# A decoder layer on one core: second batch's first attention moved in the fill, new orders of fill, loop and finish, loop written out

## The chip, the cores and the metric

The kernel runs on one core of a Trainium2 chip. The metric is the device time of one execution in microseconds (us), the median of several. The core has five engines that each work through their own queue of instructions in order: TensorE (PE, matrix products and transposes into PSUM), VectorE (DVE), ScalarE (ACT), GpSimd (POOL) and SyncE (SP, which here only issues DMAs). They meet through semaphores alone, so the order in which instructions stand in each queue is part of the program.

## What is computed

One pre-norm decoder layer over 16 batches of 256 tokens with 256 features: self-attention (16 heads of 16), cross-attention to 77 context tokens, and a soft mixture as the feed-forward (FFN), each added to its input.

```python
x = x + attn(layernorm(x))                    # 16 heads, softmax over 256 keys
x = x + xattn(layernorm(x), ctx, ctx, mask)   # 16 heads, softmax over 77 keys
# FFN: xn = rms_norm(layernorm(x)); se = rms_norm(slot_embeds)  (8 x 128 = 1024 slots)
logits   = einsum('bsd,etd->bset', xn, se)
dispatch = softmax(logits, axis=1)            # over the tokens
slots    = einsum('bsd,bset->betd', xn, dispatch)
h        = gelu(slots @ w1) @ w2              # 256 -> 1024 -> 256
combine  = softmax(logits over all 1024 slots)
x = x + einsum('bnd,bsn->bsd', h, combine)
```

## The kernel before

**Steps and prefixes.** All work is cut into some 60 named steps, each a short function per engine. A prefix tells the part: `c` is self-attention (xt.1, q, k, v, then four softmax rounds scores.n, mt.n, shifted.n, pv.n, then tr, ob, oproj), `d` is cross-attention (xt.2, kv, q2, two rounds scores2, mt2, shifted2, pv2, then tr2, ob2, oproj2) with the FFN's logits (xt.3, logits.0 to 3), `m` is the FFN in four chunks of 256 slots (lt, dispatch, slots, hidden.c.0 to 3, outer.c.0 and 1, comb, combine) and `l` its last chunk's rest, run one iteration later. In a name of the fill a number is the batch: `c1` is the second batch's self-attention. `s` are one-time steps; `s0.idle.n` is n 128x128 matmuls of the identity (line L852) whose result nobody reads.

**Order.** What stands behind what on each engine is written out by hand as lists of such names, one list per engine: START (the fill: c0 to c2, d0, d1, m0), ORDER (one iteration of the loop: c of batch b+2, d of b+1, m of b, l of b-1, 13 times, a hardware loop over `b` in `program`) and FINISH (the last two FFNs and the last cross-attention).

**A softmax round.** scores.n on PE (8 matmuls into PSUM banks 1 to 4), row maxima on DVE (`mx`, L1122, then a small copy L1125), a transpose of the maxima on PE (mt), its two halves on ACT (`mh`) and DVE (`sh`, L1130), the products again, shifted, on PE (L560, L564), exp on ACT (L895), and pv on PE (L577). The banks 1 to 4 go from user to user in a written ring, QUAD: a user may begin when the one before it has done its exp. Bank 0 goes round in a ring MISC for all short products. Banks 5 to 7 belong to the FFN: slots in 5, hidden and the transposes in 5 and 6, outer and combine in 7. c's q, k and v go to banks 1, 2 and 3 and are a user of QUAD (`c.qkv`).

**FFN precision.** Products are made of three fp32r matmuls each (`three`, L455 to L457: high x high, low x high, high x low), so each operand has a high half (ACT) and a low half (DVE, L1045 and L1255; for the hidden layer POOL, L1372). The chain of one chunk is lt, column maximum (DVE L1234), exp (ACT L955), norm (DVE L1238, L1241), dispatch, halves (ds), slots, halves (sl), hidden, gelu (ACT L991), halves (h_hi, h_lo), outer, halves (pr), combine, sum (acc).

Of the kernel before, what the change touches and what calls it, by code (L numbers as in the profile page):

```python
# [7 lines left out]
H, HD = 16, 16  # L8
# [40 lines left out]
        m.lt.0 l.outer.3.0 m.dispatch.0 d.xt.2 l.outer.3.1 c.xt.1 m.slots.0 l.comb.3 d.kv c.q m.hidden.0.0 c.k d.q2  # L49
        c.v m.hidden.0.1 d.scores2.0 m.hidden.0.2 m.hidden.0.3 m.lt.1 d.mt2.0 l.combine.3 d.shifted2.0 m.outer.0.0  # L50
        m.dispatch.1 c.scores.0 d.pv2.0 m.outer.0.1 c.mt.0 m.slots.1 m.comb.0 c.shifted.0 m.hidden.1.0 m.hidden.1.1
        c.pv.0 d.scores2.1 d.tr2.0 m.hidden.1.2 d.ob2.0 m.hidden.1.3 d.mt2.1 m.lt.2 m.combine.0 d.shifted2.1
        m.outer.1.0 m.dispatch.2 c.scores.1 d.pv2.1 m.outer.1.1 c.mt.1 m.slots.2 m.comb.1 c.shifted.1 m.hidden.2.0
# [20 lines left out]
    """,
    pool="""
        d.rstd.2 c.rstd.1 m.hid.0.0 m.hid.0.1 d.bias.2 m.hid.0.2 m.hid.0.3 m.hid.1.0 c.bias.1 m.hid.1.1 m.hid.1.2
# [6 lines left out]
        s0.idle.10 c0.xt.1 s0.idle.14 c0.q c0.k c0.v c0.scores.0 s0.idle.8 c0.mt.0 s0.idle.4 c0.shifted.0 s0.idle.6  # L83
        c0.scores.1 c0.pv.0 s0.idle.8 c0.mt.1 s0.idle.2 c0.shifted.1 s0.idle.6 c0.pv.1 s0.idle.2 c0.tr.0 c0.scores.2
        s0.idle.8 c0.ob.0 s0.idle.2 c0.mt.2 s0.idle.4 c0.shifted.2 s0.se_transp.0 s0.idle.4 c0.scores.3 c0.pv.2
        s0.idle.8 c0.mt.3 s0.idle.4 c0.shifted.3 s0.idle.4 s0.se_transp.1 c0.pv.3 s0.idle.2 c0.tr.1 s0.idle.2 c0.ob.1
        s0.idle.2 c0.oproj s0.idle.20 d0.xt.2 s0.idle.12 c1.xt.1 s0.idle.6 d0.kv c1.q c1.k d0.q2 c1.v s0.idle.4
        d0.scores2.0 s0.idle.12 d0.mt2.0 s0.idle.6 d0.shifted2.0 s0.idle.10 c1.scores.0 d0.pv2.0 s0.idle.8 c1.mt.0
        s0.idle.4 c1.shifted.0 s0.idle.2 d0.tr2.0 s0.idle.6 d0.scores2.1 c1.pv.0 s0.idle.2 d0.ob2.0 s0.idle.4
        d0.mt2.1 s0.idle.2 d0.shifted2.1 s0.idle.10 c1.scores.1 d0.pv2.1 s0.idle.8 c1.mt.1 s0.idle.2 c1.shifted.1  # L90
        s0.idle.2 d0.tr2.1 s0.idle.4 c1.pv.1 s0.idle.2 c1.tr.0 c1.scores.2 d0.ob2.1 s0.idle.2 d0.oproj2 c1.ob.0
        s0.idle.2 c1.mt.2 s0.idle.4 c1.shifted.2 s0.idle.8 c1.scores.3 c1.pv.2 s0.idle.8 c1.mt.3 s0.idle.2
        c1.shifted.3 s0.idle.8 c1.pv.3 s0.idle.2 d0.xt.3 s0.idle.4 d0.logits.0 d0.logits.1 d0.logits.2 d0.logits.3
        c1.tr.1 m0.lt.0 c1.ob.1 s0.idle.4 c1.oproj m0.dispatch.0 s0.idle.4 m0.slots.0 s0.idle.2 m0.hidden.0.0
        m0.hidden.0.1 d1.xt.2 m0.hidden.0.2 c2.xt.1 m0.hidden.0.3 d1.kv c2.q c2.k d1.q2 c2.v m0.lt.1 d1.scores2.0
        m0.outer.0.0 d1.mt2.0 m0.dispatch.1 d1.shifted2.0 m0.slots.1 m0.comb.0 c2.scores.0 d1.pv2.0 m0.outer.0.1
        c2.mt.0 m0.hidden.1.0 c2.shifted.0 d1.tr2.0 m0.hidden.1.1 d1.scores2.1 c2.pv.0 m0.hidden.1.2 d1.ob2.0
        d1.mt2.1 m0.lt.2 m0.hidden.1.3 d1.shifted2.1 m0.combine.0 m0.dispatch.2 c2.scores.1 d1.pv2.1 m0.slots.2
        c2.mt.1 m0.comb.1 c2.shifted.1 m0.outer.1.0 c2.pv.1 c2.scores.2 d1.tr2.1 m0.outer.1.1 d1.ob2.1 m0.hidden.2.0
        c2.tr.0 m0.hidden.2.1 d1.oproj2 m0.hidden.2.2 c2.ob.0 m0.hidden.2.3 m0.lt.3 c2.mt.2 m0.combine.1 c2.shifted.2  # L100
        m0.outer.2.0 m0.dispatch.3 c2.scores.3 c2.pv.2 m0.slots.3 m0.comb.2 c2.mt.3 m0.outer.2.1 c2.shifted.3
        m0.hidden.3.0 m0.hidden.3.1 c2.pv.3 m0.hidden.3.2 d1.xt.3 m0.combine.2 m0.hidden.3.3 d1.logits.0 d1.logits.1
# [3 lines left out]
        c0.xt.1 s0.hi.0 s0.hi.1 c0.q c0.mh.0 c0.ex.0 s0.se_squares c0.xo.0 c0.mh.1 c0.ex.1 c0.xo.1 c0.od.0 c0.mh.2
        c0.ex.2 c0.xo.2 c0.mh.3 s0.hi.2 s0.se_hi.0 c0.ex.3 c0.xo.3 s0.hi.3 c0.od.1 d0.xt.2 c1.xt.1 c1.q s0.se_hi.1
        d0.q2 d0.mh2.0 d0.ex2.0 d0.xo2.0 c1.mh.0 s0.hi.4 c1.ex.0 c1.xo.0 d0.od2.0 d0.mh2.1 d0.ex2.1 d0.xo2.1 c1.mh.1
        c1.ex.1 c1.xo.1 d0.od2.1 c1.od.0 c1.mh.2 c1.ex.2 c1.xo.2 c1.mh.3 c1.ex.3 c1.xo.3 d0.xt.3 d0.logits.0
# [1425 lines left out]
```

## Time and profile before

| | us |
|---|---|
| median of 3 runs (1885.05 to 1885.58) | 1885.53 |
| the profiled execution's own time | 1885.74 |
| its span, first to last instruction | 1883.9 |
| PE busy in the span | 1817.1 (96%) |
| DVE, ACT, POOL busy | 1071.3, 969.7, 426.4 |
| fill, to the loop's first instruction on PE | 258.6 |
| loop, 13 iterations | 1449.7 |
| finish | 175.6 |

The profile is one execution read by the hardware profiler. Its page gives each engine's busy time and the costliest groups of instructions. The trace behind it answers questions: instructions in order of time, who waited for whom, busy time by stretch. Rows of PE overlap a little, since matmuls are pipelined and their ends are modelled. An x16 on an fp32 product of 8 matmuls, or x20 on 10 fillers, is right: each shows as two.

### The profile page before, as it was taken

The numbers are of one execution on the slowest core, as the hardware profiler recorded it, in microseconds if no ns is written. First come the engines' busy times: TensorE is split into PE (matmuls) and PEld (weight loads), VectorE is DVE, ScalarE is ACT, GpSimd is POOL, SyncE is SP. The second block draws the span as 40 slices with busy tenths as digits, with TensorE's granted clock in tenths as the row PEclk, the third lists the DMA queues.
The fourth block names the chain that finished last, engine by engine and source line by source line (L and its number), as shares of the span: only waits on it lengthen the run. The fifth ranks groups of instructions, "written<-read, shape, count | busy, mean of one in ns | idle before, by whom it ended". The sixth has DMA issues, their size and how long they took to land.

```text
span 1883.9 us, 42647 instructions
## 1 busy us (share of the span) xinstructions
PE 1817.1 (96%) x17464; PEld 1621.7 (86%) x17464; DVE 1071.3 (57%) x2211; ACT 969.7 (51%) x1711; POOL 426.4 (23%) x351
## 2 busy tenths in 40 slices
PE   8999999999999999999999999999999999999998
PEld 7878898898989889898888989889898988989888
DVE  3445565665655556565665656556565655655453
ACT  3334646555454554555455554555546455555653
POOL 2011222221221222121222122122122122212232
PEclk9999999999999999999999999999999999999999
DMA  4000000000000000000000000000000000000000
GB/s 153 9 1 9 2 10 7 7 9 1 15 1 7 9 2 15 1 9 7 7 9 1 15 1 10 7 7 9 1 15 1 9 7 7 9 1 7 1 7 6
DMA packets 20842, 19.75 MB, mean 10 GB/s; under 512 B 9920, under 2 KB 19776, under 8 KB 20288
## 3 DMA queue, kind: packets, MB, share of 16 engines
q1 hardware_dynamic: 20672, 17.06, 3.2%
q8 instruction: 158, 2.59, 0.6%
q14 instruction: 12, 0.10, 0.0%
HBM read 12.86 MB, written 4.19 MB: 9 GB/s over the span
## 4 chain that ended last, share of the span: by engine, by line
PE 66%; issue 19%; DVE 7%; POOL 5%; ACT 3%; POOLq 0%; DMA 0%; DVEq 0%; SPq 0%; ACTq 0%
PE ps L455 14%; PE ps L457 13%; PE ps L456 13%; POOL h_lo L1372 4%; PE ps L540 3%; PE ps L852 3%; PE ps L577 2%; PE ps L671 2%; PE ps L717 2%; PE ps L687 2%; PE ps L652 1%; PE ps L760 1%; DVE h_hi L1255 1%; POOL pw_d L1356 1%; DVE sl_lo L1045 1%
## 5 line engine op out<-in xcount | busy, mean ns | idle before, releaser
L1372 POOL TENSOR_TENSOR h_lo<-h_f,h_hi 128x512 fp32r<-128x512 f32 x256 | 331.6, 1297 | 1120.5 <-DVE h_hi L1255 1120.5
L455 PE MATMUL ps<-sl_hi,w_hi 128*128 128x256 f32 x1024 | 302.3, 295 | 11.8 <-DVE cb_lo L1045 9.9
L455 PE MATMUL ps<-w_hi,h_hi 128*128 128x256 f32 x1024 | 301.3, 294 | 3.9 <-POOL h_lo L1372 3.9
L456 PE MATMUL ps<-w_hi,h_lo 128*128 128x256 f32 x1024 | 290.0, 283 | 0.0
L457 PE MATMUL ps<-w_lo,h_hi 128*128 128x256 f32 x1024 | 290.0, 283 | 0.0
L456 PE MATMUL ps<-sl_hi,w_lo 128*128 128x256 f32 x1024 | 289.1, 282 | 0.0
L457 PE MATMUL ps<-sl_lo,w_hi 128*128 128x256 f32 x1024 | 289.0, 282 | 0.0
L1255 DVE CAST h_hi<-h_f 128x512 fp32r<-128x512 f32 x256 | 132.6, 520 | 218.1 <-ACT h_f L991 217.6
L991 ACT ACTIVATE h_f<-ps 128x512 f32<-128x512 f32 x256 | 152.4, 596 | 136.4 <-PE ps L457 135.3
L1122 DVE TENSOR_REDUCE mx<-ps 128x8 f32<-128x2048 f32 x64 | 146.5, 2289 | 131.8 <-PE ps L540 131.8
L455 PEld LDWEIGHTS ps<-w_hi,h_hi 128*128 128x128 f32 x1024 | 196.0, 191 | 29.0 <-issue 24.1
L455 PEld LDWEIGHTS ps<-sl_hi,w_hi 128*128 128x128 f32 x1024 | 194.8, 190 | 25.5 <-issue 20.4
L456 PEld LDWEIGHTS ps<-w_hi,h_lo 128*128 128x128 f32 x1024 | 196.5, 192 | 0.0
L457 PEld LDWEIGHTS ps<-w_lo,h_hi 128*128 128x128 f32 x1024 | 196.3, 192 | 0.0
L456 PEld LDWEIGHTS ps<-sl_hi,w_lo 128*128 128x128 f32 x1024 | 195.4, 191 | 0.1
L457 PEld LDWEIGHTS ps<-sl_lo,w_hi 128*128 128x128 f32 x1024 | 195.1, 191 | 0.0
L895 ACT ACTIVATE pt<-ps 128x2048 f32<-128x2048 f32 x64 | 120.4, 1881 | 47.6 <-PE ps L564 47.6
L866 ACT ACTIVATE xo<-ps 128x512 f32<-128x512 f32 (+1 forms) x96 | 43.7, 455 | 150.7 <-PE ps L687 92.5
L866 ACT ACTIVATE mh<-ps 128x512 fp32r<-128x512 f32 (+1 forms) x96 | 43.6, 454 | 99.0 <-PE ps L549 84.2
L991 ACT ACT_TABLE_LOAD x67 | 86.0, 1283 | 10.3 <-PE ps L457 9.1
L866 ACT ACTIVATE od<-ps 128x256 f32<-128x256 f32 x64 | 24.6, 384 | 122.8 <-PE ps L596 70.1
L866 ACT ACTIVATE pr_hi<-ps 128x512 fp32r<-128x512 f32 x64 | 38.3, 599 | 89.0 <-PE ps L457 89.0
(202 smaller groups left out, 4225.8 us busy)
## 6 DMA issues: line engine op xcount, KB each, us to landing
x<-in_x SPq DMA_DIRECT2D x16, 256.0 KB, 2.7
out<-acc SPq DMA_DIRECT2D x16, 256.0 KB, 2.2
g_w<-in_w SPq DMA_DIRECT2D x2, 1024.0 KB, 11.4
...
```

What stands on the lines that cost most here:

```text
L455: te.matmul(o, lhs[0], rhs[0], start=first, stop=False)
L456: te.matmul(o, lhs[1], rhs[0], start=False, stop=False)
L457: return te.matmul(o, lhs[0], rhs[1], start=False, stop=last)
L540: last = te.matmul(ps[:, 1 + i, t * S:(t + 1) * S], q[rows, c, t * P:(t + 1) * P], km[rows, e, c, :], start=True, stop=True)
L577: last = te.matmul(ps[32 * i:32 * i + 32, 0, 0:S], vz[:, j, 8 * c + 2 * i + e, :], pt[:, i, j, :], start=j == 0, stop=j == NT - 1)
L852: te.matmul(ps[:, 7, 0:P], ident[:, :], ident[:, :], start=True, stop=True)
L866: return nc.scalar.activation(o, i, ACT.Copy)
L895: nc.scalar.activation(pt[:, :, :, :].rearrange("p i j s -> p i (j s)"), ps[:, 1:1 + R, :], ACT.Exp)\
L991: nc.scalar.activation(h_f[:, 2 * q:2 * q + 2, :], halves(hidden_bank(b, q)), ACT.Gelu).then_inc(s["ge"], 1)
L1122: V.tensor_reduce(mx[:, n, :, :], ps[:, 1:1 + R, :].rearrange("p i (t s) -> p i t s", t=NT), AX, ALU.max, negate=True).then_inc(s["mx"], 1)
L1255: V.tensor_copy(h_hi[:, 2 * q:2 * q + 2, :], h_f[:, 2 * q:2 * q + 2, :]).then_inc(s["h_hi"], 1)
L1372: Q_.tensor_tensor(h_lo[:, part, :], h_f[:, part, :], h_hi[:, part, :].bitcast(f32), ALU.subtract)\
```

## The change

What it does:

- **Fill.** c1's q, k and v go to banks 5, 6 and 7 instead of 1 to 3 (`qkv_bank`), which the FFN has not used yet, and leave the ring QUAD. Their evictions on ACT and DVE get one wait more each (for c0's last products), and the first batch's lt, slots and outer wait for them (`km`, `q_sb`, `v_sb` of batch 1). In QUAD_START d0's two users now stand ahead of all four of c1's, and d0's logits ahead of c1's third and fourth. c1's steps stand later, d0's and m0's earlier. The fillers go from 276 to 183. The slot embeddings' transposes (se_transp) are cut from two steps over two banks into four over bank 5.
- **All three lists** of PE, ACT, DVE and POOL are new; k now stands ahead of q. Each holds the same steps as before, save those split ones and the fillers. nrm and nrm2 wait for ob and ob2 of the half before.
- **The loop** of 13 iterations is a Python loop: the same instructions, written out one after another, with constants in the waits instead of registers.

PE in the fill, from c0's oproj on (L607 before, L613 after; L852 and L865 are the fillers, L497 and L500 xt, wkv the step kv). Before:

```order
L607 MATMUL ps<-wo,od 128x256 x4
L852 MATMUL ps<-consts 128x128 x20
L497 MATMUL ps<-consts,xh_d 128x128 x4
L852 MATMUL ps<-consts 128x128 x12
L497 MATMUL ps<-consts,xh_a 128x128 x4
L852 MATMUL ps<-consts 128x128 x6
L618 MATMUL ps<-wkv_61,cx 77x256 x2
L621 MATMUL ps<-cx,wkv_61 128x77 x4
L455 MATMUL ps<-xa_hi,wqk_hi 128x256
```

After:

```order
L613 MATMUL ps<-wo,od 128x256 x4
L857 MATMUL ps<-consts,g_se 128x128 x4
L865 MATMUL ps<-consts 128x128
L624 MATMUL ps<-wkv_61,cx 77x256 x2
L627 MATMUL ps<-cx,wkv_61 128x77 x4
L865 MATMUL ps<-consts 128x128 x8
L500 MATMUL ps<-consts,xh_d 128x128 x4
L857 MATMUL ps<-consts,g_se 128x128 x4
L865 MATMUL ps<-consts 128x128 x3
L458 MATMUL ps<-xd_hi,wq_hi 128x256
```

c1's transpose (xh_a) and its projections (wqk) are gone from between d0's xt.2 and d0's q2, and 26 fillers less stand there.

DVE in the fill, from d0's first row maxima on (mx_107, md_108, sh_110, rl_112 are cross-attention's tiles; mx, md, sh self-attention's). Before:

```order
L1177 TENSOR_REDUCE mx_107<-ps 128x16
L1180 COPY md_108<-mx_107 128x32
L1186 SCALAR_TENSOR_TENSOR sh_110<-mh_109,consts,ps 128x512
L1122 TENSOR_REDUCE mx<-ps 128x8
L1125 COPY md<-mx 128x16
L1130 SCALAR_TENSOR_TENSOR sh<-mh,consts,ps 128x256
L1193 RECIPROCAL rl_112<-ps 128x16
L1196 TENSOR_TENSOR on_113<-ps,rl_112 128x8x16 x2
L1177 TENSOR_REDUCE mx_107<-ps 128x16
```

After:

```order
L1198 TENSOR_REDUCE mx_107<-ps 128x16
L1201 COPY md_108<-mx_107 128x32
L1106 TENSOR_SCALAR xh_a<-x,mv,pw 128x256 x2
L1207 SCALAR_TENSOR_TENSOR sh_110<-mh_109,consts,ps 128x512
L1060 TENSOR_TENSOR xa_lo<-ps,xa_hi 128x512
L1198 TENSOR_REDUCE mx_107<-ps 128x16
```

c1's first softmax round (L1122, L1130) no longer stands between d0's two rounds.

PE in the loop, from the FFN's lt.3 (tile lg) to dispatch.3 (tile edt); wo_63 is oproj2. Before:

```order
L751 MATMUL ps<-consts,lg 128x128 x4
L717 MATMUL ps<-wo_63,od_114 128x256 x4
L455 MATMUL ps<-pr_hi,cb_hi 128x256
...
L549 MATMUL ps<-consts,md 128x128 x2
L760 MATMUL ps<-consts,edt 128x128 x4
```

After:

```order
L759 MATMUL ps<-consts,lg 128x128 x4
L723 MATMUL ps<-wo_63,od_114 128x256 x4
L566 MATMUL ps<-q,km 128x256 x4
L570 MATMUL ps<-sh,ones 128x256 x4
...
L583 MATMUL ps<-pt,vz 32x256 x8
L458 MATMUL ps<-w_hi,h_hi 128x256
...
L593 MATMUL ps<-consts,xo 128x128 x4
L768 MATMUL ps<-consts,edt 128x128 x4
```

Where combine.1 (12 matmuls) stood behind oproj2, shifted.2, pv.1, outer.2.0 (24 matmuls) and tr.0 stand now, and combine.1 stands earlier.

The core of the diff; of the lists, only the loop's PE list around the place above is shown. In order: the list, the ring, the loop, `qkv_bank` and its users on PE, the new waits of the first lt, slots and outer, those of the evictions of c1's q, k and v, those of nrm and nrm2 (the same two lines with ob2's semaphore), and SyncE's loop:

```diff
-        c.pv.1 c.scores.2 d.tr2.1 m.hidden.2.1 d.ob2.1 m.hidden.2.2 c.tr.0 m.hidden.2.3 c.ob.0 m.lt.3 d.oproj2
-        m.combine.1 c.mt.2 m.dispatch.3 c.shifted.2 m.comb.2 m.slots.3 c.scores.3 c.pv.2 m.outer.2.0 c.mt.3
+        m.hidden.2.1 d.tr2.1 c.scores.2 m.combine.1 d.ob2.1 m.hidden.2.2 c.mt.2 m.hidden.2.3 m.lt.3 d.oproj2
+        c.shifted.2 c.pv.1 m.outer.2.0 c.tr.0 m.dispatch.3 c.scores.3 c.pv.2 m.slots.3 m.comb.2 c.mt.3 m.outer.2.1
...
 QUAD_START = """
-    c0.qkv c0.quad.0 c0.quad.1 c0.quad.2 c0.quad.3 c1.qkv d0.oct.0 c1.quad.0 d0.oct.1 c1.quad.1 c1.quad.2 c1.quad.3
-    d0.logits c2.qkv d1.oct.0 c2.quad.0 d1.oct.1 c2.quad.1 c2.quad.2 c2.quad.3 d1.logits
+    c0.qkv c0.quad.0 c0.quad.1 c0.quad.2 c0.quad.3 d0.oct.0 d0.oct.1 c1.quad.0 c1.quad.1 d0.logits c1.quad.2
+    c1.quad.3 c2.qkv c2.quad.0 d1.oct.0 d1.oct.1 c2.quad.1 c2.quad.2 c2.quad.3 d1.logits
...
     run_list(steps, START[engine])
-    with handle.Fori(1, B - 2) as b:
-        run(engine, steps, c=b + 2, d=b + 1, m=b, l=b - 1)
+    for b in range(1, B - 2):
+        run(steps, ORDER[engine], c=b + 2, d=b + 1, m=b, l=b - 1)
     run_list(steps, FINISH[engine])
...
+        def qkv_bank(a, k):
+
+            return (5, 6, 7)[k] if second_batch(a) else 1 + k
...
             def q_step(a):
 
+                if second_batch(a):
+                    pe.wait_ge(s["i_slo"], 2 * ND)
...
             def k_step(a):
 
                 split(a, "wqk")
-                quad_free("c.qkv", a)
+                if not second_batch(a):
+                    quad_free("c.qkv", a)
                 pe.wait_ge(s["xt1_lo"], nth("xt1_lo", a, 1))
...
+                    if not later(b):
+                        pe.wait_ge(s["km"], nth("km", 1, 1))
...
+                    if not later(b):
+                        pe.wait_ge(s["q_sb"], nth("q_sb", 1, 1))
...
+                    else:
+                        pe.wait_ge(s["v_sb"], nth("v_sb", 1, 1))
...
+                if second_batch(a):
+                    act.wait_ge(s["st_ps"], nth("st_ps", a - 1, Q))
...
+                if second_batch(a):
+                    dve.wait_ge(s["st_ps"], nth("st_ps", a - 1, Q))
...
+                if second_batch(a):
+                    dve.wait_ge(s["pv"], nth("pv", a - 1, Q))
...
+                if c:
+                    dve.wait_ge(s["ob_ps"], nth("ob_ps", a, c))
...
-            with sp.Fori(1, B - 3) as b:
+            for b in range(1, B - 3):
```

## Rows read from the trace of the kernel before

**Rows 1.** The page: busy us, share of the span, instructions, by engine.

```profile
PE 1817.1 (96%) x17464; PEld 1621.7 (86%) x17464; DVE 1071.3 (57%) x2211; ACT 969.7 (51%) x1711; POOL 426.4 (23%) x351
```

**Rows 2.** Stretches from:to, length, busy us by engine, PE clock: fill, loop, finish.

```profile
3.85:258.61 254.76, 241.31 (x2380) 208.72 (x2381) 122.96 (x258) 111.13 (x181) 44.47 (x34) 1.00 0.10 31
...
258.61:1708.34 1449.73, 1415.87 (x13730) 1261.08 (x13729) 860.79 (x1781) 770.82 (x1365) 333.81 (x273) 1.00 0.03 7
1708.34:1883.90 175.56, 159.95 (x1357) 151.89 (x1355) 87.10 (x171) 86.47 (x164) 45.61 (x35) 0.99 0.02 6
```

**Rows 3.** Groups of instructions: busy us, mean ns, idle before; the fillers.

```profile
L852 PE MATMUL ps<-consts 128*128 128x128 f32 x552 | 74.4, 285 | 3.9 <-DMA consts<-in_consts 3.9
```

**Rows 4.** PE by time (start, us, line, tiles): c0's scores.0, .1, .3.

```profile
17.84 1.15 PE L540 MATMUL ps<-km,q 32*128 32x256 f32 x16 [1.16 <-DVE vz L1115]
...
26.46 1.15 PE L540 MATMUL ps<-km,q 32*128 32x256 f32 x16 [0.44 <-ACT pt L895]
...
46.08 1.15 PE L540 MATMUL ps<-km,q 32*128 32x256 f32 x16
```

**Rows 5.** The same view: c0.oproj, d0.scores2.0, d0.oproj2, d0.logits.0, m0.hidden.0.0.

```profile
59.09 1.96 PE L607 MATMUL ps<-wo,od 128*128 128x256 f32 x8
...
79.06 0.41 PE L645 MATMUL ps<-mk_r,ones 1*128 1x308 f32 x4
...
120.63 1.97 PE L717 MATMUL ps<-wo,od 128*128 128x256 f32 x8
...
141.54 0.47 PE L455 MATMUL ps<-se_hi,xd_hi 128*128 128x512 f32 x1 [0.57 <-issue]
...
156.62 0.39 PE L455 MATMUL ps<-sl_hi,w_hi 128*128 128x256 f32 x1 [0.97 <-DVE sl_lo L1045]
```

**Rows 6.** PE's waits: us in all, times, longest; first two loop only, then all.

```profile
PE ps L760 <- DVE edt L1241: 15.9, 13, 1.2
...
PE ps L455 <- DVE cb_lo L1045: 9.2, 26, 0.4
...
PE ps L497 <- DVE xh_d L1091: 3.4, 13, 0.3
PE ps L824 <- DVE ds_lo L1045: 2.5, 13, 0.2
```

**Rows 7.** PE by time: two FFN matmuls in a row; lt.3 and dispatch.3 of one iteration.

```profile
280.67 0.28 PE L456 MATMUL ps<-sl_hi,w_lo 128*128 128x256 f32 x1
280.79 0.28 PE L457 MATMUL ps<-sl_lo,w_hi 128*128 128x256 f32 x1
...
780.27 0.60 PE L751 MATMUL ps<-consts,lg 128*128 128x128 f32 x4
...
785.78 0.66 PE L760 MATMUL ps<-consts,edt 128*128 128x128 f32 x4 [1.23 <-DVE edt L1241]
```

**Rows 8.** DVE and POOL by time: row maxima of d's round 0, their copy; copy of round 1.

```profile
726.76 1.44 DVE L1177 TENSOR_REDUCE mx<-ps 128x16 f32<-128x1232 f32 x1
...
728.08 1.29 POOL L1366 TENSOR_TENSOR x<-x,biases 128x512 f32<-128x512 f32 x1
...
728.24 1.18 DVE L1180 COPY md<-mx 128x32 f32<-128x32 f32 x1
...
753.92 0.20 DVE L1180 COPY md<-mx 128x32 f32<-128x32 f32 x1
```

**Rows 9.** PE's waits in the finish.

```profile
PE ps L455 <- POOL h_lo L1372: 3.9, 3, 1.8
PE ps L760 <- DVE edt L1241: 1.8, 1, 1.8
```

**Rows 10.** Code fetches from 400 to 512 us (packets, MB, engines' share); PE across an iteration's end.

```profile
q8 instruction: 10, 0.16, 0.7%
...
814.52 1.89 PE L607 MATMUL ps<-wo,od 128*128 128x256 f32 x8
816.26 0.65 PE L751 MATMUL ps<-consts,lg 128*128 128x128 f32 x4
```

More of the change, by code:

```diff
@@ L48 @@
     pe="""
[L49 to L53, printed above, removed]
@@ L82 @@
     pe="""
[L83 to L102, printed above, removed]
@@ new lines @@
+        s0.idle.3 c0.ob.1 s0.idle.2 c0.oproj s0.se_transp.1.0 s0.idle.1 d0.kv s0.idle.8 d0.xt.2 s0.se_transp.1.1
+        s0.idle.3 d0.q2 s0.idle.4 d0.scores2.0 s0.idle.8 d0.mt2.0 s0.idle.6 d0.shifted2.0 c1.xt.1 s0.idle.6
+        d0.scores2.1 d0.pv2.0 c1.k d0.mt2.1 c1.q d0.shifted2.1 d0.tr2.0 c1.v d0.ob2.0 c1.scores.0 d0.pv2.1 s1.idle.3
+        d0.tr2.1 s1.idle.4 c1.mt.0 s1.idle.4 d0.ob2.1 c1.shifted.0 d0.oproj2 s1.idle.1 c1.scores.1 c1.pv.0 s1.idle.6
+        c1.mt.1 s1.idle.5 c1.shifted.1 s1.idle.3 d0.xt.3 s1.idle.7 d0.logits.0 d0.logits.1 d0.logits.2 d0.logits.3
@@ new lines @@
+        s1.idle.3 m0.lt.0 c1.scores.2 c1.pv.1 s1.idle.6 c1.mt.2 s1.idle.2 m0.dispatch.0 c1.shifted.2 c1.tr.0
+        m0.slots.0 c1.ob.0 c1.scores.3 c1.pv.2 m0.hidden.0.0 c1.mt.3 m0.hidden.0.1 c1.shifted.3 d1.kv m0.hidden.0.2
+        s1.idle.1 c1.pv.3 s1.idle.2 c1.tr.1 m0.hidden.0.3 c1.ob.1 m0.lt.1 c1.oproj m0.outer.0.0 m0.dispatch.1 d1.xt.2
+        m0.outer.0.1 c2.xt.1 m0.slots.1 m0.comb.0 c2.k c2.q c2.v m0.hidden.1.0 c2.scores.0 d1.q2 m0.hidden.1.1
+        c2.mt.0 m0.hidden.1.2 c2.shifted.0 m0.hidden.1.3 d1.scores2.0 c2.pv.0 m0.lt.2 d1.mt2.0 m0.combine.0
@@ new lines @@
+        d1.shifted2.0 m0.outer.1.0 m0.dispatch.2 d1.scores2.1 d1.pv2.0 m0.outer.1.1 d1.mt2.1 m0.slots.2 m0.comb.1
+        d1.shifted2.1 d1.tr2.0 m0.hidden.2.0 d1.ob2.0 c2.scores.1 m0.hidden.2.1 m0.hidden.2.2 c2.mt.1 m0.hidden.2.3
+        d1.pv2.1 c2.shifted.1 m0.lt.3 d1.tr2.1 m0.combine.1 d1.ob2.1 c2.scores.2 c2.pv.1 m0.dispatch.3 d1.oproj2
+        m0.comb.2 c2.mt.2 m0.slots.3 c2.shifted.2 m0.outer.2.0 c2.tr.0 c2.scores.3 c2.pv.2 m0.outer.2.1 c2.mt.3
+        m0.hidden.3.0 c2.shifted.3 d1.xt.3 m0.hidden.3.1 m0.hidden.3.2 m0.combine.2 c2.pv.3 d1.logits.0 c2.ob.0
@@ L104 @@
+        m0.hidden.3.3 c2.tr.1 d1.logits.1 d1.logits.2 c2.ob.1 d1.logits.3 c2.oproj
     """,
     act="""
[L106 to L109, printed above, removed]
```

298 lines of the change are left out of this document (154 added, 144 removed).

## The prediction

> **What bounds the kernel.** The page's busy times come first: PE works 1817.1 of 1883.9 us, DVE 57%, ACT 51% [rows 1]. Where PE has work ready, a matmul of 256 columns follows the last after 0.12 us [rows 7]. So the kernel can get shorter only where PE idles or does work that nobody reads. The second view, three stretches side by side, shows where that is [rows 2]: fill 254.76 us with 241.31 busy; loop 1449.73 with 1415.87 busy, so 33.9 idle, 2.6 in each of 13 iterations of 111.5; finish 175.56 with 159.95 busy. The third, the groups of instructions, shows that the fill's 241.31 are no real load: 276 fillers take 74.4 of it, 0.27 us each [rows 3]. The fill's length is set by chains of dependent steps across the engines. Its marks on PE, read from the instructions in time, are c0.oproj 59.09, d0.scores2.0 79.06, d0.oproj2 120.63, d0.logits.0 141.54, m0.hidden.0.0 156.62 [rows 5] and the loop's start 258.61 [rows 2].
>
> The sum is made against the profiled execution's 1885.74 us (span 1883.9 and 1.8 outside it); the median, 1885.53, is 0.2 lower.
>
> **Fill.** Six legs, one mark to the next. One turn of the ring of banks (scores, maxima, mt, shifted, exp) takes 26.46 - 17.84 = 8.62 us [rows 4].
>
> 1. To c0.oproj, 59.09. The fourth round begins at 46.08 now, behind se_transp.0 and fillers; three bare turns behind the first it would begin at 17.84 + 3 x 8.62 = 43.7. In the new list scores.3 has tr.0 and 5 fillers ahead of it and se_transp is cut in four. I take the bare turn: -2.4, oproj at 56.7.
> 2. To scores2.0, 19.97 now. Ahead of it 26 fillers go (26 x 0.27 = 7.0) and c1's xt.1, q, k, v. These are 4 transposes and 36 matmuls at 0.12, some 4.9 us, part of which now only fills a wait for d0's projections; with both gone the chain oproj, x1, statistics, xh, transpose, q2 is left bare. I take -8.6, leaving 11.4: less than the 11.9 taken out, because the bare chain then binds. scores2.0 at 68.0.
> 3. To oproj2, 41.57 now. c1.quad.0 and c1.quad.1 leave the ring between d0's users: two turns of about 8.6 less, and 0.8 comes back where c1's q, k and v stand between d0's steps. I take -16.4, leaving 25.2; oproj2 at 93.2.
> 4. To logits.0, 20.9 now, with c1.quad.2 and quad.3 in the ring ahead of it; now the bank ring puts one c1 turn there (quad.1, with quad.0 begun before oproj2). One turn less: -8.8, logits.0 at 105.3.
> 5. To hidden.0.0, 15.1 now. c1's scores.2, shifted.2, mt.2 and scores.3 stand inside this leg, 0.6 to 1.2 each, beside the exp and norm that bind it: +2.6, hidden.0.0 at 123.
> 6. To the loop, 102.0 now. This stretch is matmul-bound already; c1's last round, tr.1, ob.1 and oproj move into it, which is 8 fp32 matmuls each of shifted, pv and oproj beside small ones, 4.7 us, and 1.0 of new waits: +5.7, loop at 231.
>
> Sum -2.4 - 8.6 - 16.4 - 8.8 + 2.6 + 5.7 = -27.9; I take **-27**. Another road bounds it: 93 fillers less are 93 x 0.27 = 25.1 us, and the fill idles 254.76 - 241.31 = 13.5 now, so more than -31 would need nearly half that idle gone too. The low end, -22, has two things the walk may have wrong: POOL's s0.lo.4 stands just ahead of d0.rstd.2, and ACT's s0.hi.4 and s0.se_hi.1 near od.1 and xt.2; each is a weight's half that took no path before. No row prices their meeting; the nearest, the DVE copy below that met POOL and took 1.0 longer [rows 8], would put it at 1 us a meeting, five of them at 5.
>
> **Loop.** PE's waits, grouped by what ended them [rows 6], give 31 of the 33.9 us idle less the small ones. Four groups are broken by the new order:
> dispatch.3 on the norm (edt), 15.9 in 13: lt.3 begins at 780.27 and dispatch.3 at 785.78, 5.5 us of chain of which 1.23 is wait [rows 7]. The new order puts oproj2 (1.7, a 1.97 with its overlap [rows 5]), shifted.2 and pv.1 (1.3 and 1.0, like the 1.15 of scores [rows 4]), outer.2.0 (24 x 0.12 = 2.9 [rows 7]) and tr.0 (0.4) there, with lt itself 8 us: the chain is covered, -15.9.
> hidden.1.0 and 2.0 on cb_lo, 9.2 in 26: outer.0.1 and outer.1.1 (2.9 each) now stand between comb and it. -9.2.
> xt.2 on xh_d, 3.4 in 13: xt.2 now stands behind slots.0, some 5 us later, against a longest wait of 0.3. -3.4.
> comb.2 on ds_lo, 2.5 in 13: scores.3, pv.2 and slots.3 stand between. -2.5.
> These are 31.0, 2.4 an iteration. PE also pays at each wait for the lost overlap of pipelined matmuls; the spans in a row show 0.28 for a start each 0.12 [rows 7], so up to 0.16 per wait, of which there are some five an iteration: 0.8 more at most. Against it stand the new waits. I walked one iteration's four queues with the durations of the trace. shifted.3 finds sh.3 0.2 late, since d.xt.3 (0.4) took over from longer work; on DVE d.mx2.0 now stands ahead of hid.0.1 to 0.3 and of cm.1, so POOL's casts (1.3 each, as the 1.29 row [rows 8]) end with 0.5 to spare for outer.0.0; some ten more links have under 0.1. I put them at 0.3 where they add, and take back 0.2 of the overlap's 0.8: 2.4 + 0.2 - 0.3 = 2.3 an iteration, **-30**, period 109.2. Upper bound: all of 33.9 and the overlap, -41. Lower bound: each of the ten tight links 0.1 late, 1.0, and a copy's 1.0 worse each iteration: 2.3 - 2.0, -4; I hold -12 for the range, since not all links can be on the path at once.
>
> The last of these bounds has its row: DVE's copy after the maxima took 1.18 us where POOL's tensor operation had begun 0.16 before it, and 0.20 where not [rows 8]. In the new order the same copy comes some 1 us after POOL's operation ends, by my walk. The Trainium skill, "SBUF — State Buffer", section "SBUF: two separate sides", calls the port pair that the two share an exclusive lock held for a whole instruction; the trace agrees, with 1.29 against 1.18. By that rule, if the order shifts the copy by a microsecond, the loop would lose 1.0 x 13 = 13 us of the 30.
>
> Written out, the loop has the same instructions and no branch. Code comes at 10 packets in 112 us, 0.7% of 16 engines, so 0.007 x 16 x 112 / 10 = 1.25 us each [rows 10]. PE passes an iteration's end from c.oproj at 814.52 to lt at 816.26: 1.74 for a matmul group that lasts 1.89, no gap [rows 10]. I take 0. The added waits for c1's q, k, v and for ob are on things long done (oproj of c0 is 13 us ahead of c1's eviction by the marks): 0, bounded by the smallest wait group above, 0.2 each.
>
> **Finish.** dispatch.3 of the last but one FFN waits 1.8 on edt [rows 9]; oproj2 and outer.2.0 (1.7 + 2.9) now stand ahead of it: -1.8. The last FFN's outer.0.0 waits for POOL's h_lo, a part of the 3.9 in three [rows 9], 1.3; it moves behind dispatch.2: -1.2. The end stays. **-3**, between -6 (all 5.7 of both rows) and 0.
>
> **Sum.** 1885.7 - 27 - 30 - 3 = 1825.7, or **1825.5** against the median.
>
> **Rivals.** *A, the forecast*, 0.72; own range 1812 (ends -31, -37 and -6) to 1840.
> *B, the loop's waits only change places.* The order is a balance of four queues; ten links with under 0.1 to spare speak for it, and that idle is only 2.6 an iteration. Against it speaks that the covers are 2 to 3 us where the waits are 0.2 to 1.2. Then 1885.5 - 27 - 3 = 1855.5. 0.16.
> *C, the branch had a price.* If each engine had to fetch the loop's first code anew at each turn, writing it out would save 13 x 1.25 = 16 us more: about 1809. No gap at the iteration's end speaks against it. 0.04. The Trainium skill, "Runtime: NRT & Kernel Launch", section "Instruction fetch mechanics", says that a taken branch to code outside the current window must fetch before it goes on, and that full unrolling is preferred for it; the 1.74 us above do not show it.
> *D, the change doesn't do what it says in the fill*: d0's chain is as long without c1's turns, since the engines' own chain binds it, not the ring. Then only loop and finish remain, 1885.5 - 33 = 1852.5. Against it, 41.57 us for two cross-attention rounds is nearly five turns. 0.05.
> *E, slower: code comes late.* At 10 packets per 112 us the span needs about 168; if the written-out code were not fetched ahead, each would stop its engine for 1.25 us: 168 x 1.25 = 210 us, time 1885.5 - 60 + 210 = 2035. It decides from 60 / 1.25 = 48 packets on, 2 in 7. Against it: fill and finish are straight code already, and the fill idles 13.5 us in 2380 groups of matmuls [rows 2], too little for late code. 0.03.
>
> **Numbers.** Faster by over 0.2% (3.8 us, about what a measurement of this kernel tells from no change): A, B, C, D less a sliver, 0.95. Same 0.02, slower 0.03. The range 1812 to 1852 leaves out C, E, and most of B, 0.2 together.
>
> **What would show it.** PE's marks: c0.oproj about 57, scores2.0 68, oproj2 93, logits.0 105, hidden.0.0 123, loop from 231. Leg 3 is the test of the ring: if it is still over 35, D holds. 183 fillers. A period of 109.2, with no wait on edt or cb_lo and under 0.6 us of PE idle an iteration; if the idle is over 2 under other names, B. Finish 172. Code packets at the same rate; gaps of 1 us in several engines that nothing in the trace ends would be E, a period below 108 would be C. The forecast is wrong above all if the hand walk missed a link: one 1 us link in the loop is 13 us.

## The result, and the profile after

The changed kernel takes 1810.32 us (median of 4 runs, 1810.08 to 1810.62) against 1885.55 (4 runs, 1885.05 to 1885.74): ratio 0.9601, 95% interval 0.9585 to 0.9618. That is 75.2 us less, where 60 were forecast, and 1.7 us below the low end of the range.

The page of after, its busy line (compare [rows 1]), and, in the second block, the three stretches, cut at the same steps as [rows 2] (from:to, length, busy us with counts for PE, PEld, DVE, ACT, POOL, then PE clock, DMA share, GB/s):

```profile
PE 1781.7 (99%) x17278; PEld 1596.0 (88%) x17278; DVE 1062.4 (59%) x2213; ACT 970.0 (54%) x1713; POOL 429.9 (24%) x351
```

```profile
3.70:233.02 229.32, 220.72 (x2194) 187.39 (x2195) 124.16 (x260) 116.39 (x187) 44.40 (x34) 1.00 0.11 34
233.02:1637.82 1404.80, 1402.99 (x13730) 1258.15 (x13729) 850.49 (x1781) 770.15 (x1366) 337.89 (x274) 1.00 0.03 7
1637.82:1808.50 170.68, 158.03 (x1357) 150.49 (x1355) 87.27 (x171) 82.16 (x160) 45.14 (x35) 1.00 0.02 6
```

The loop began at 258.61 and begins at 233.02: 25.6 us less. The loop went from 1449.73 to 1404.80 with the same 13730 matmul records: 44.9 less, a period of 108.06 instead of 111.5. The finish went from 175.56 to 170.68: 4.9 less. The sum is 75.4 of span. PE's busy time in the loop fell only from 1415.87 to 1402.99, so 32 of the 44.9 us were idle on record and 13 were not. What is left of idle in the loop is 1.8 us in all.

PE in order of time (start, us, engine, line, tiles), the marks of the fill and the seam of two iterations of the loop; in the second block the fillers' group (183 fillers, 50.8 us):

```profile
56.71 0.46 PE L613 MATMUL ps<-wo,od 128*128 128x256 f32 x1
...
68.50 0.42 PE L651 MATMUL ps<-mk_r,ones 1*128 1x308 f32 x4
...
94.03 0.48 PE L723 MATMUL ps<-wo,od 128*128 128x256 f32 x1
...
107.17 0.47 PE L458 MATMUL ps<-se_hi,xd_hi 128*128 128x512 f32 x1
...
125.02 0.39 PE L458 MATMUL ps<-sl_hi,w_hi 128*128 128x256 f32 x1
...
772.85 0.59 PE L613 MATMUL ps<-wo,od 128*128 128x256 f32 x2
773.28 0.38 PE L759 MATMUL ps<-consts,lg 128*128 128x128 f32 x2
```

```profile
L865 PE MATMUL ps<-consts 128*128 128x128 f32 x366 | 50.8, 287 | 3.7 <-DMA consts<-in_consts 3.7
```

Against [rows 5] the first five are c0.oproj (59.09 before), scores2.0 (79.06), oproj2 (120.63), logits.0 (141.54) and hidden.0.0 (156.62). The next view, PE's waits over the whole span by what ended them, has nothing of edt left, and cb_lo and xh_d only outside the loop:

```profile
PE ps L458 <- POOL h_lo L1396: 4.6, 6, 2.1
PE ps L865 <- DMA consts<-in_consts: 3.7, 1, 3.7
PE ps L500 <- DVE xh_d L1106: 1.7, 2, 1.2
PE ps L458 <- DVE sl_lo L1060: 1.5, 2, 1.0
...
PE ps L458 <- DVE cb_lo L1060: 0.4, 1, 0.4
```

### The profile page after: what moved, and what is told of

Its sections match the earlier page's. It is cut to its first block, busy times and chain, and to the rows that moved or that the text cites. A ratio compares the mean times of both kernels' runs of the same rounds, so it can differ in the third digit from the quotient of the medians.

```text
span 1808.5 us, 40567 instructions
## 1 busy us (share of the span) xinstructions
PE 1781.7 (99%) x17278; PEld 1596.0 (88%) x17278; DVE 1062.4 (59%) x2213; ACT 970.0 (54%) x1713; POOL 429.9 (24%) x351
## 4 chain that ended last, share of the span: by engine, by line
PE 91%; DVE 4%; POOL 3%; ACT 2%; issue 1%; DMA 0%; POOLq 0%; DVEq 0%; SPq 0%; ACTq 0%
PE ps L458 22%; PE ps L459 20%; PE ps L460 20%; PE ps L546 4%; PE ps L566 3%; POOL h_lo L1396 3%; PE ps L583 2%; PE ps L677 2%; PE ps L693 2%; PE ps L836 2%; PE ps L658 2%; PE ps L768 1%; PE ps L613 1%; PE ps L759 1%; PE ps L500 1%; DVE h_hi L1278 1%
## 5 line engine op out<-in xcount | busy, mean ns | idle before, releaser
L1396 POOL TENSOR_TENSOR h_lo<-h_f,h_hi 128x512 fp32r<-128x512 f32 x256 | 336.2, 1323 | 1125.8 <-DVE h_hi L1278 1125.8
L1278 DVE CAST h_hi<-h_f 128x512 fp32r<-128x512 f32 x256 | 156.7, 622 | 118.0 <-ACT h_f L1006 117.6
L1060 DVE TENSOR_TENSOR ds_lo<-ps,ds_hi 128x512 fp32r<-128x512 f32 x64 | 44.1, 688 | 90.5 <-ACT ds_hi L879 90.4
L879 ACT ACTIVATE ds_hi<-ps 128x512 fp32r<-128x512 f32 x64 | 38.2, 597 | 104.3 <-PE ps L768 104.2
L970 ACT ACTIVATE edt<-ps,cm 128x256 f32<-128x256 f32 x128 | 59.6, 470 | 60.6 <-DVE cm L1257 58.9
```

Of the source, the lines that this page charges most:

```text
L879: return nc.scalar.activation(o, i, ACT.Copy)
L970: last = nc.scalar.activation(edt[:, e, :], ps[:, 6, e * S:(e + 1) * S], ACT.Exp, bias=cm[:, k:k + 1], accum_out=csum[:, k:k + 1])
L1278: V.tensor_copy(h_hi[:, 2 * q:2 * q + 2, :], h_f[:, 2 * q:2 * q + 2, :]).then_inc(s["h_hi"], 1)
L1396: Q_.tensor_tensor(h_lo[:, part, :], h_f[:, part, :], h_hi[:, part, :].bitcast(f32), ALU.subtract)\
```

## The experiments

Each run was measured together with the kernel before on the same chip, and that one's median was 1885.8 to 1886.3, against 1885.55 above. So medians of different runs can be set side by side to about 1 us. The letters are the theories of the expectations, and C is the prediction's rival.

**Is it the order or the writing out?** First the two changes to the loop one at a time. e1 is the kernel before with Python loops, e2 the changed kernel with the hardware loop, e3 the kernel before with the loop's new lists.

```diff
# e1, on the kernel before (e2 is the same in reverse, on the changed kernel)
-    with handle.Fori(1, B - 2) as b:
+    for b in range(1, B - 2):
...
-            with sp.Fori(1, B - 3) as b:
+            for b in range(1, B - 3):
# e3, on the kernel before: ORDER, MISC and QUAD of the changed kernel, and in nrm (nrm2 alike)
+                if c:
+                    dve.wait_ge(s["ob_ps"], nth("ob_ps", a, c))
```

> The kernel before with its loop written out in Python, every list as before. Theory W (what a wait costs PE is its recorded idle plus the overlap that the pipelined matmuls lose at it, 3.44 us an iteration in all; branch, registers and code fetch cost nothing): 1885.5, within 1. Rival H (the 0.84 us an iteration by which the loop got shorter beyond its recorded idle came from the hardware loop's branch and register waits): 1885.5 - 11 = 1874.6. The prediction's rival C: 1869.

> The changed kernel with the hardware loop put back on all engines, orders as in the changed one. Theory W: 1810.3, within 1, period 108.06. Rival H: 1810.3 + 11 = 1821, period 108.9. Rival C: 1826.

> The kernel before with the loop's four lists, both bank rings of the loop and nrm's wait as in the changed kernel; fill, finish and the hardware loop as before. Theory W: the whole loop gain and nothing else, 1885.5 - 44.9 = 1840.6, within 2 for the two seams; PE's period 108.06 and no idle in it. Rival H: 0.84 an iteration stays, 1851.5, period 108.9. If the fill's new end is needed for a loop without waits (its steps reach the loop late otherwise), the first iterations are longer than the rest.

Measured: e1 1886.7 against 1885.9, ratio 1.0001 (0.9992 to 1.0011): writing out the old order does nothing. e2 1843.4: in the changed kernel the hardware loop costs 33 us. e3 1864.7: the new order in a hardware loop brings 21.2 of the 44.9. By e3's trace its loop takes 1428.8 us against 1404.8, so behind the old fill the hardware loop costs 24. The branch is taken 12 times: 2.75 us each in e2, 2.0 in e3. What makes the two differ was not found; 6.1 us of gaps inside outer.3.0 stand in e2 alone. No theory foresaw any of this: H and C priced the branch alike in both orders, W at nothing. PE's waits from the second to the last iteration, in e3 and in e2 (us in all, times, longest), then the seam in e2:

```profile
PE ps L753 <- issue: 19.6, 12, 1.9
```

```profile
PE ps L767 <- issue: 19.7, 12, 1.9
PE ps L468 <- issue: 6.1, 8, 1.0
```

```profile
780.27 0.38 ACT L887 ACTIVATE od<-ps 128x256 f32<-128x256 f32 x1
...
781.23 1.89 PE L621 MATMUL ps<-wo,od 128*128 128x256 f32 x8
784.86 0.65 PE L767 MATMUL ps<-consts,lg 128*128 128x128 f32 x4 [1.74 <-issue]
```

L753 and L767 are lt, the first step behind the branch. "issue" says that no semaphore released it. Before, the same seam had none: 814.52, then 816.26 [rows 10]. Here lt comes 4.2 us after od.1 (780.65), the last thing that a step ahead of the branch waits for. In the kernel before there were 5.3 us from od.1's end (810.99) to lt, so a price of about 4.2 could lie under work that PE had queued.

The DMA view agrees that code is fetched there. In e2, e3, e5, e9 and the kernel before, one packet of instructions moves 2.6 to 3.0 us ahead of lt at each of the 19 seams looked at (in e2, 2.9 ahead of 784.86; in the kernel before, 2.9 ahead of 816.26); at seven seams of e1 and of the changed kernel none moves between 4 and 2 us ahead of it. So the fetch is there in the kernel before too, under matmuls. No run changes the fetch alone, so that it is what lt waits for rests on this timing.

e5 tests whether queued work can cover the price: in e2, od.1 early again.

```diff
-        d.logits.1 d.logits.2 d.logits.3 c.ob.1 m.combine.2 c.oproj
+        d.logits.1 c.ob.1 d.logits.2 d.logits.3 m.combine.2 c.oproj
...
-        m.ge.3.3 m.ec.3 d.logits.0 d.logits.1 d.logits.2 d.logits.3 c.od.1
+        m.ge.3.3 c.od.1 m.ec.3 d.logits.0 d.logits.1 d.logits.2 d.logits.3
```

> As e2 (changed orders, hardware loop), with c.ob.1 moved ahead of logits.2 on PE and c.od.1 ahead of ec.3 on ACT, so that what c.oproj, the last step before the branch, waits for is done some 5 us before PE needs it, as in the kernel before (od.1 ended 5.3 us ahead of the next lt there, 4.2 in e2). Theory Q (PE's sequencer may not go past the wait of c.oproj early; only what PE still has queued by then covers the fetch behind the branch): the 1.74 us gap at lt goes, 1843.4 - 13 x 1.9 = 1819; 1812 if outer.3.0's stretch (4.36 instead of 3.12 us) goes too. Rival D (the branch empties PE's queue and costs the same wherever the waits are; the order before hid it otherwise): 1843.

Measured 1825.6: 17.8 us less, so where the wait stands does matter and rival D is out; but the gap only shrank. PE's waits in the loop, and the seam:

```profile
PE ps L766 <- issue: 8.2, 12, 1.0
```

```profile
775.02 1.89 PE L620 MATMUL ps<-wo,od 128*128 128x256 f32 x8
777.84 0.54 PE L766 MATMUL ps<-consts,lg 128*128 128x128 f32 x3 [0.93 <-issue]
```

od.1 now ended at 771.41, 6.4 us ahead of lt, and yet 0.68 us is left on average. So time since the last wait isn't all; what differs still from before is which matmuls stand last: combine.2 of 256 columns instead of logits of 512. e9 puts these last.

```diff
-        d.logits.1 c.ob.1 d.logits.2 d.logits.3 m.combine.2 c.oproj
+        d.logits.1 c.ob.1 m.combine.2 d.logits.2 d.logits.3 c.oproj
```

> As e5 (changed orders, hardware loop, od.1 early), with combine.2 moved ahead of logits.2, so that logits.2, logits.3 (6 matmuls of 512 columns each, 1.37 us) and c.oproj stand last before the branch, as in the kernel before. Theory Q2 (before a branch PE's sequencer can be ahead by a fixed number of instructions, not by a time; about 20 matmuls. In e5 the last 20 are oproj and combine.2, 1.7 + 1.4 = 3.2 us, against 4.2 from the last wait to lt in e2; before, they are oproj and two logits, 4.5 us): the gap at lt goes, 1825.6 - 13 x 1.0 = 1812.5. Rival D2 (a fixed cost of about 1 us is left in any order that has no slack elsewhere): 1825.

Measured 1822.4, not 1812.5. The gap at lt did go: "issue" fell from 8.2 us in 12 to one of 0.3, elsewhere.

```profile
PE ps L465 <- DVE pr_lo L1067: 2.2, 11, 0.2
PE ps L467 <- issue: 0.3, 1, 0.3
```

```profile
1211.01 1.89 PE L620 MATMUL ps<-wo,od 128*128 128x256 f32 x8
1213.03 0.54 PE L766 MATMUL ps<-consts,lg 128*128 128x128 f32 x3
```

The run is slower than expected because combine.2, now earlier, waits for pr_lo (0.2 each, and 0.16 of overlap lost with it), lt still begins 2.02 us after oproj where 1.74 is bare, and from lt to kv it takes 3.66 us instead of 3.31. These add to 1.0, and the period (109.01) is 0.95 above 108.06. The fixed number of instructions in Q2 fits three kernels' seams (none, 0.68, near none), but a queue's depth was only inferred from them; the 0.35 behind lt was not taken apart.

**What a wait costs.** e6 puts one long wait back into the changed kernel, e13 a short one.

```diff
# e6
-        c.shifted.2 c.pv.1 m.outer.2.0 c.tr.0 m.dispatch.3 c.scores.3
+        c.shifted.2 m.dispatch.3 c.pv.1 m.outer.2.0 c.tr.0 c.scores.3
# e13
-        m.slots.0 d.xt.2 c.k c.q m.hidden.0.0 d.q2
+        m.slots.0 d.xt.2 c.k m.hidden.0.0 c.q d.q2
```

> The changed kernel with dispatch.3 moved ahead of pv.1, outer.2.0 and tr.0 in the loop's PE list, so that it waits for the norm again: edn.3 ends at 744.5, shifted.2 would end at 742.6. Theory W (a wait costs its recorded idle and 0.16 to 0.25 of lost overlap): idle about 1.9 recorded, period longer by 2.1, 1810.3 + 13 x 2.1 = 1838. Rival I (a wait costs what is recorded, as the prediction all but took it): period longer by just the recorded idle. The comparison of period and recorded idle decides, whatever the wait's size is.

Measured 1844.8, 34.5 more than the changed kernel, 2.65 an iteration. PE's waits in iterations 2 to 12, and the stretches of four iterations (as above):

```profile
PE ps L768 <- DVE edt L1264: 21.3, 11, 2.0
```

```profile
234.09:345.66 111.57, 109.63 (x1057) 97.74 (x1056) 65.32 (x137) 59.48 (x106) 26.23 (x22) 0.98 0.03 7
345.66:455.69 110.03, 108.09 (x1057) 96.75 (x1056) 65.20 (x137) 59.11 (x105) 25.98 (x21) 1.00 0.03 7
455.69:567.23 111.54, 109.61 (x1058) 97.85 (x1057) 65.32 (x137) 59.11 (x105) 25.96 (x21) 0.98 0.03 7
567.23:677.26 110.03, 108.09 (x1057) 96.75 (x1056) 65.29 (x137) 59.11 (x105) 25.98 (x21) 1.00 0.03 7
```

The wait is 1.94 each. Iterations at clock 1.00 are 1.97 longer than 108.06; those at 0.98, 6 of 13, are 3.5 longer: right behind the wait, in the 3.7 us from 314.01 on, the granted clock is 0.54 of full, so nearly all of it at TensorE's lower level of 1.2 GHz instead of 2.4; pv.1 and outer.2.0 take 1.5 us more. No theory had that. The period by itself doesn't separate W from I, since a small wait of outer.2.0 vanished with the move: it now begins 1.00 us after pv.1's start, and 1.20 in the changed kernel. With this 0.20 put back, the wait of 1.94 costs 2.17, W's 2.1 and not I's 1.94.

> The changed kernel with hidden.0.0 moved ahead of c.q in the loop's PE list. It then waits for sl_lo, which ends some 0.65 us after c.k does. Theory W (price is recorded idle plus the overlap of 0.16 us that the pipelined matmuls have without a wait): recorded 0.65, period longer by 0.81, 1810.3 + 10.5 = 1820.8, clock 1.00 throughout. Rival I (price is the recorded idle): period longer by 0.65, 1818.8. Rival S (the later steps make it up): 1810.

Measured 1822.5, and 1811.1 for the changed kernel beside it: 11.3 more, 0.87 an iteration. PE's waits in 12 iterations, one iteration's hidden.0.0, the granted clock over most of the loop; then the same place in the changed kernel:

```profile
PE ps L458 <- DVE sl_lo L1060: 7.6, 12, 0.6
```

```profile
681.44 0.39 PE L458 MATMUL ps<-sl_hi,w_hi 128*128 128x256 f32 x1 [0.63 <-DVE sl_lo L1060]
```

```profile
366.00:1528.00 1162.00, 1154.08 (x11321) 1031.06 (x11320) 696.88 (x1453) 635.57 (x1124) 274.83 (x223) 1.00 0.03 7
```

```profile
679.04 0.28 PE L460 MATMUL ps<-xa_lo,wqk_hi 128*128 128x256 f32 x1
679.16 0.28 PE L458 MATMUL ps<-sl_hi,w_hi 128*128 128x256 f32 x1
```

The period went from 108.06 to 108.97, 0.91, for 0.63 of recorded idle. Of the other 0.28, 0.16 is the overlap (a matmul starts 0.12 after the last one, whose record is 0.28 long), and 0.11 is the first matmul behind the wait, 0.39 instead of 0.28. I and S are out; W has the right mechanism and is too small.

**The fill.** e7 drops all fillers of the changed kernel (every `idle` name from START's PE list), e8 halves them in the kernel before, e10 puts c1's projections back into the ring.

```diff
# e8 (each n of s0.idle.n halved, rounded down)
-        s0.idle.10 c0.xt.1 s0.idle.14 c0.q c0.k c0.v c0.scores.0 s0.idle.8 c0.mt.0
+        s0.idle.5 c0.xt.1 s0.idle.7 c0.q c0.k c0.v c0.scores.0 s0.idle.4 c0.mt.0
# e10, on the changed kernel (on ACT c1.q, on DVE c1.k also stand one place later)
-            return (5, 6, 7)[k] if second_batch(a) else 1 + k
+            return 1 + k
...
-                if not second_batch(a):
-                    quad_free("c.qkv", a)
+                quad_free("c.qkv", a)
...
-    c0.qkv c0.quad.0 c0.quad.1 c0.quad.2 c0.quad.3 d0.oct.0 d0.oct.1 c1.quad.0
+    c0.qkv c0.quad.0 c0.quad.1 c0.quad.2 c0.quad.3 d0.oct.0 d0.oct.1 c1.qkv c1.quad.0
...
-        d0.scores2.1 d0.pv2.0 c1.k d0.mt2.1 c1.q d0.shifted2.1 d0.tr2.0 c1.v d0.ob2.0 c1.scores.0
+        d0.scores2.1 d0.pv2.0 s0.idle.8 d0.mt2.1 s0.idle.8 d0.shifted2.1 d0.tr2.0 d0.ob2.0 c1.k c1.q c1.v c1.scores.0
```

> The changed kernel without its 183 fillers (matmuls of the identity whose result nobody reads). Theory C (they hold TensorE's granted clock up while PE waits): the clock in the fill falls to its lower level for part of it, PE's steps on the chain take twice as long there, 5 to 20 us more, 1815 to 1830. Rival P (they only fill waits): 1810, within 1. Rival L (they lengthen the chain where they are over-long): 1807 to 1809.

Measured 1830.4, 20 more; the loop starts at 254.15, and its period is unchanged. The stretches of the fill, the clock third from the right:

```profile
3.93:40.00 36.07, 19.90 (x144) 14.72 (x148) 14.00 (x32) 10.99 (x26) 9.55 (x7) 0.77 0.59 186
40.00:80.00 40.00, 29.15 (x195) 18.81 (x192) 17.81 (x38) 13.88 (x18) 5.23 (x2) 0.63 0.04 10
80.00:120.00 40.00, 29.03 (x323) 21.08 (x321) 19.98 (x41) 12.28 (x17) 3.77 (x4) 0.80 0.01 1
120.00:160.00 40.00, 33.44 (x268) 25.47 (x261) 19.30 (x41) 19.96 (x29) 4.33 (x4) 0.84 0.00 1
```

The fillers are there for the clock: theory C, at the top of its range.

> The kernel before with each filler step cut to half, 138 fillers instead of 276. If the fillers are load and removing 93 of them was worth 25.1 us by itself: 1885.5 - 37 = 1848. If they lie inside waits and their number follows from the chains' length: 1885.5, within 1. If half of them no longer hold the clock: 1886 to 1900.

Measured 1881.9, 3.9 less (ratio 0.9983, 0.9974 to 0.9993), and in the profiled execution (1879.9) the clock is 1.00 all through the fill. So the fillers aren't load (1848 is out), but a few were over-long: c0.scores.0 began at 16.59 instead of 17.84 [rows 4], and the loop at 254.3. In the ten executions time and mean clock go together, from 1879.2 at 1.00 to 1885.3 at 0.995: half the fillers hold the clock in some executions and not in others. Of the long ones only time and mean clock are on record, so where in the kernel it fell is not known.

> The changed kernel with c1's q, k and v in banks 1 to 3 again, as a user of the ring between d0's second round and c1's first (on PE behind d0's ob2.0, 16 fillers in their old places). If the banks 5 to 7 matter, c1's first scores come later by exp, projections and evictions, some 4 to 5 us (86.5 to 91), and with them logits.0 and the loop: 1815. If only the order of the ring's users matters and the banks not: 1811.

Measured 1816.0, 5 to 6 more: the banks matter. c1's first scores, here and in the changed kernel:

```profile
92.31 0.50 PE L545 MATMUL ps<-km,q 32*128 32x256 f32 x4 [0.79 <-DVE vz L1133]
```

```profile
86.47 0.50 PE L546 MATMUL ps<-km,q 32*128 32x256 f32 x4
```

The loop began at 238.88 instead of 233.02. So of the fill's 25.6 us the new banks, with the places that they allow c1's projections, carry about 5.8. No run tests the rest part by part; the order of the ring's users fits it by leg 3 below, 41.57 us before and 25.5 after.

**The finish.** e4 is the changed kernel with FINISH and MISC_FINISH of before.

> The changed kernel with the finish's lists and its bank ring as before. If the finish's own order brings its 4.9 us: 1815.2. If that gain comes from the state in which the new loop leaves the queues: 1810.5.

Measured 1815.5, 5.2 more than 1810.3, though its runs spread from 1812.9 to 1817.0. So the gain comes from the finish's own order, not from the state in which the loop leaves the queues. Its size is less sure: in e4's trace, the execution of 1812.9, the finish takes 174.18 us, 3.5 more than the changed kernel's 170.68, with PE idle 15.7 against 12.65. The same lists took 175.56 in the kernel before, whose last outer.3.0 ran partly at the lower level behind a wait of 1.77 (0.60 of full from 1868.4 to 1872.5); in e4's trace the clock did not fall behind the same wait. So about 3.0 of the 4.9 us are idle, and 1.5 are matmuls that were slow in that one execution.

**Two repairs.** e11 moves one name in POOL's START list; e12 adds three more edits.

```diff
-        c0.rstd.1 c0.bias.1 s0.se_scale s0.lo.4 d0.rstd.2 c1.rstd.1 d0.bias.2 d0.rstd.3 c1.bias.1
+        c0.rstd.1 c0.bias.1 s0.se_scale s0.lo.4 d0.rstd.2 c1.rstd.1 d0.bias.2 c1.bias.1 d0.rstd.3
# e12 also (and m-1.hid.3.2, m-1.hid.3.3 leave POOL's FINISH list)
-        d0.x2 c1.mx.1 d0.stats.3
+        d0.x2 d0.stats.3 c1.mx.1
...
-        s0.idle.8 c0.xt.1 s0.idle.18 c0.k c0.q c0.v s0.idle.3 c0.scores.0
+        s0.idle.5 c0.xt.1 s0.idle.7 c0.k c0.q c0.v s0.idle.2 c0.scores.0
...
+                if last_batch(b) and n >= 14:
+                    dve.wait_ge(s["h_hi"], nth("h_hi", b, n + 1))
+                    part = slice(2 * q, 2 * q + 2)
+                    V.tensor_tensor(h_lo[:, part, :], h_f[:, part, :], h_hi[:, part, :].bitcast(f32), ALU.subtract)\
+                        .then_inc(s["h_lo"], 1)
```

> The changed kernel with POOL's c1.bias.1 moved ahead of d0.rstd.3. In the trace of the changed kernel it runs at 102.27 to 103.54, beside DVE's d0.xh.3 at 102.33, which takes 2.60 us instead of the 1.4 to 1.5 of other xh. Theory L (the two engines held each other up): xh.3 takes 1.4, xt.3 and logits.0 come up to 1.1 us earlier, unless the ring (c1.ex.1 ends at 104.9) and 7 fillers take it: 1809.3 to 1810.3. Rival (xh.3 is long for another reason): no change in its length.

In the changed kernel, POOL and DVE ahead of d0.xh.3:

```profile
102.27 1.27 POOL L1390 TENSOR_TENSOR x<-x,biases 128x512 f32<-128x512 f32 x1
...
102.33 1.23 DVE L1094 TENSOR_TENSOR sc<-pw_d 128x2 f32<-128x2 f32 x1 [0.75 <-POOL pw_d L1380]
```

In e11:

```profile
102.72 0.16 DVE L1094 TENSOR_TENSOR sc<-pw_d 128x2 f32<-128x2 f32 x1 [0.75 <-POOL pw_d L1380]
```

An operation on two elements a partition took 1.23 us beside POOL's and 0.16 alone: L holds, and xt.3's wait of 1.20 became 0.13. From c0.scores.0 to the loop the trace is 0.9 shorter. The time is 1811.2 (1809.1 to 1811.5), which can't be told from the changed kernel's.

> A version meant to be faster than the changed kernel: c1.bias.1 as in e11; d0.stats.3 ahead of c1.mx.1 on DVE; the first fillers cut from 8, 18 and 3 to 5, 7 and 2 (with 5 and 7, c0.scores.0 began at 16.59 in e8 instead of 17.9); and of the last hidden chunk the third and fourth low halves made by DVE right behind its cast instead of by POOL (the last outer waits 2.07 us for them now). Expected 1.2 from the start, 1.0 from logits.0, 1.2 from the end: 1807. If the clock falls with fewer fillers at the start: 1811 or more.

Measured 1808.1, where 1807 was expected. Both kernels once more on one chip:

> The changed kernel once more, beside e13 and e15: 1810.3, within 1.

> The trimmed kernel of e12 once more: if its gain is real, 2 to 3 us below e14 on the same chip; if it came from the call, within 0.5.

e14 1811.1, e15 1808.4: the trimmed kernel is 2.7 us faster than the changed one on the same chip, 0.15%. c0.scores.0 begins 1.75 earlier (16.16) and the loop 2.1 earlier (230.94). The last outer's wait fell only from 2.07 to 1.68, since it is then acc, not h_lo, that comes last.

## Why the prediction was off, step by step

*Fill, -27 forecast, -25.6 measured.* The walk leg by leg held: to c0.oproj 56.7 forecast, 56.71 measured; to scores2.0 11.4 and 11.8; to oproj2 25.2 and 25.5; to logits.0 12.1 and 13.1; to hidden.0.0 17.7 and 17.85; to the loop 107.7 and 108.0. The largest miss, 1.0 in leg 4, is DVE's 1.23 beside POOL, which the text had priced at 1 us a meeting, but expected elsewhere. In e11, without that meeting, logits.0 comes 0.9 earlier. Rival D is out by leg 3. The cross-check by 93 fillers x 0.27 came near for the wrong reason: by e8, 138 fillers less were worth 3.9 us. Their number follows the chain's length and doesn't set it.

*Loop, -30 forecast, -44.9 measured.* Here the range broke. The mechanism was right: the four groups of waits went, 31.0 us, and no new one over 0.2 came. Wrong were two terms, both on one side. The step that failed is the overlap lost at a wait. It was bounded at 0.16 per wait and 0.8 an iteration, and then 0.2 was taken without a reason. Measured, PE's busy time fell by (1415.87 - 1402.99) / 13 = 0.99 an iteration, which is 0.20 for each of the five waits, between the 0.16 of overlap alone and e13's 0.28 with the slow first matmul; so this term carries 13 x 0.79 = 10.3 of the 14.9 us missed. At these five waits themselves it was not taken apart: that it is overlap and slow restart is carried over from e6 and e13, and that it is not the branch is shown by e1. The second is the 0.3 of new waits: the loop has 1.8 us of idle left in all 13 iterations, 0.14 each. A small third: idle outside the four groups, 2.6 against 2.4, went too. So 2.6 - 0.14 + 0.99 = 3.45 an iteration stands where 2.4 - 0.3 + 0.2 = 2.3 was taken. The range broke for one reason more. Its bound for "all of 33.9 and the overlap" was given as -41, but by its own terms it is 33.9 + 13 x 0.8 = 44.3, and the low end then took -37 for the loop, for which it gives no reason. With -44.3 the low end would have been 1804.

*Written out, 0 forecast.* For the old order right (e1). In this change it did not spoil the sum, since the order's gain was worked out with no gap at the seam, but as a price for the branch it was wrong: with the new lists in the hardware loop the kernel takes 1843 (e2). [Rows 10] showed no gap at the seam, which said that the branch was covered, not that it was free; the new order takes the cover away, and the unrolling is what keeps the order's gain. Rival C named the mechanism but gave it as a saving on top, at 1.25 a turn; measured in the new order it is 1.64 at lt, and 2.0 (e3) to 2.75 (e2) in all. The Trainium skill, "Runtime: NRT & Kernel Launch", section "Instruction fetch mechanics", says that a taken branch to code outside the window must fetch before it goes on; e2 and e3 agree, with a gap of 1.64 us at lt. [Rows 10] beside e1, e5 and e9 add that the stall can be hidden nearly or wholly.

*DVE beside POOL.* The loop's 26 md copies took 0.195 to 0.204 us, as where one ran alone before (0.20 [rows 8]), so the 13 us on the lock did not come. The lock itself showed in the fill: 1.23 against 0.16. The Trainium skill, "SBUF — State Buffer", section "SBUF: two separate sides", names a DVE instruction with two inputs in SBUF, beside a GpSimd one that reads SBUF, among those that contend for the pair. The trace agrees, even for two elements a partition.

*Finish, -3 forecast, -4.9 measured,* inside its 0 to -6. The wait on edt went, as forecast, 1.8. The 1.2 on POOL's h_lo did not: PE waits 4.1 us for it in the finish now, 3.9 before [rows 9]. Waits on ACT's od and DVE's on went instead, 1.1 in all. The idle fell by 3.0, so that this sum came out right is partly luck, and 1.5 of the rest is the clock (e4).

*Rivals B and E* are out: no wait took another's place, and from 400 to 512 us code comes at 9 packets on the queue that had 10, and 2 on another, with no gap on PE.
